# Feed-forward columns regrouped by batch in a fused attention and feed-forward kernel: the first group's opening chunks move into the cross attention, its norm onto the gate products

## The reference, cut to what matters

```python
cctx = sdpa(cq, ck, cv, causal=False)                       # 16 heads of 16
cctx = cctx.transpose(0, 2, 1, 3).reshape(b, l, CC)          # CC = 256
hidden_states = hidden_states + cctx @ cdense_w              # "dense" below
mi = rms_norm(hidden_states, ln_post_attn_w)                 # mean square over the 512 channels
v_out = jax.nn.silu(mi @ v_gate) * (mi @ v_up) @ v_down      # hidden width I = 1376
l_out = jax.nn.silu(mi @ l_gate) * (mi @ l_up) @ l_down
hidden_states = hidden_states + jnp.where(vm, v_out, l_out)
```

## Time and profile before

| what | us |
|---|---|
| three runs | 2171.53, 2175.74, 2179.38 (median 2175.74) |
| the profiled execution, and its span from first to last instruction | 2180.68, 2178.7 |
| PE busy over the span | 1996.9 (92%) |
| DVE, ACT, POOL busy | 1523.9, 1007.2, 509.4 |
| feed-forward, from its first instruction to the end of the span | 1682.3 to 2178.7 |

### The profile page before, as it was taken

One profiled execution on the slowest core, in us unless ns is written; L12 is line 12 of the kernel. 1 busy time (PEld: TensorE's weight loads), 2 busy tenths in 40 slices (PEclk: granted clock), 3 DMA queues, 4 the chain that ended last, 5 costly groups with the idle time before them and its releaser, 6 DMA issues. The chain is left out here.

```text
span 2178.7 us, 32799 instructions
## 1 busy us (share of the span) xinstructions
PE 1996.9 (92%) x12654; PEld 1340.6 (62%) x12654; DVE 1523.9 (70%) x2111; ACT 1007.2 (46%) x1748; POOL 509.4 (23%) x496
## 2 busy tenths in 40 slices
PE   6999997799979997788879999999998799999997
PEld 5788875677845554676634444444434677878885
DVE  5676776588847775656579999999952565766563
ACT  1232314455425554444348888888884222221111
POOL 0321231133401222332201312223222212221211
PEclk9999998799969999999979999999999899999998
DMA  3222112333377663685545344354401333334332
GB/s 139 71 99 80 35 57 78 121 122 122 101 189 175 169 151 103 205 254 201 154 114 96 68 89 87 73 98 78 91 14 40 112 92 99 102 109 114 94 97 56
DMA packets 174793, 236.92 MB, mean 109 GB/s; under 512 B 26218, under 2 KB 103022, under 8 KB 172426
## 3 DMA queue, kind: packets, MB, share of 16 engines
q1 hardware_dynamic: 166480, 223.65, 38.3%
q0 software_dynamic: 7856, 10.90, 1.8%
q10 hardware_dynamic: 288, 0.08, 0.0%
HBM read 169.54 MB, written 62.91 MB: 107 GB/s over the span
## 5 line engine op out<-in xcount | busy, mean ns | idle before, releaser
L2120 ACT ACTIVATE pT_x<-ps 128x512 f32<-128x512 f32 (+1 forms) x832 | 451.3, 595 | 84.6 <-PE ps L2218 57.0
L2159 DVE TENSOR_REDUCE quarters<-ps 128x2 f32<-128x804 f32 x480 | 454.1, 992 | 45.5 <-PE ps L2190 44.7
L2233 PE MATMUL ps<-pT_x,vx_ring 128*17 128x256 f32 (+1 forms) x3328 | 261.5, 387 | 0.2 <-ACT osb_x L2102 0.2
L105 PE MATMUL ps<-mi_h,w_hi 128*128 128x512 f32 (+1 forms) x440 | 174.0, 395 | 12.8 <-DVE mi_l L2414 12.8
L2379 POOL TENSOR_TENSOR sg<-sg,keep_all 128x512 f32<-128x512 f32 (+1 forms) x55 | 88.1, 1602 | 386.0 <-ACT sg L2358 386.0
L106 PE MATMUL ps<-mi_h,w_lo 128*128 128x512 f32 (+1 forms) x440 | 173.2, 394 | 0.0
L107 PE MATMUL ps<-mi_l,w_hi 128*128 128x512 f32 (+1 forms) x440 | 173.1, 393 | 0.0
L1307 DVE TENSOR_REDUCE row_max_s<-ps 128x1 f32<-128x384 f32 (+3 forms) x176 | 109.4, 633 | 68.6 <-PE ps L1339 67.8
L1279 ACT ACTIVATE pT_s<-ps 128x512 f32<-128x512 f32 (+1 forms) x176 | 96.0, 558 | 117.6 <-PE ps L1364 115.6
L99 DVE CAST w_hi<-w_raw 128x512 fp32r<-128x512 f32 (+1 forms) x165 | 84.3, 511 | 72.4 <-PE ps L107 65.4
L2233 PEld LDWEIGHTS ps<-pT_x,vx_ring 128*17 128x17 f32 (+1 forms) x3328 | 55.6, 95 | 110.7 <-issue 68.8
(11 more groups left out here) (350 smaller groups left out, 4821.0 us busy)
## 6 DMA issues: line engine op xcount, KB each, us to landing
qkv_l<-self_q_by_part SPq DMA_DIRECT2D x48, 256.0 KB, 4.4
qkv_h<-self_k_by_part SPq DMA_DIRECT2D x48, 256.0 KB, 6.7
w_raw<-L_xattn_l_gate SPq DMA_DIRECT2D x40, 256.0 KB, 2.9
w_raw<-L_xattn_l_up SPq DMA_DIRECT2D x40, 256.0 KB, 2.9
w_raw<-L_xattn_l_down SPq DMA_DIRECT2D x40, 256.0 KB, 2.7
kx_first<-cross_k_by_part SPq DMA_DIRECT2D x36, 200.2 KB, 7.2
cross_v_by_group<-v_aug SPq DMA_DIRECT2D x16, 442.0 KB, 3.9
vx_ring<-cross_v_by_group SPq DMA_DIRECT2D x16, 442.0 KB, 10.1
```

Of the source, the lines that this page charges most:

```text
L105: nc.tensor.matmul(dst, ah, bh, start=start, stop=False, **how)
L2120: nc.scalar.activation(pT[0:kn, u % 3, j, :], ps[0:kn, 5 + v % 3, :], ACT.Exp, scale=SCALE)\
L2159: nc.vector.tensor_reduce(out=quarters[:, g % 2, pair, :, q, quarter], in_=ps[:, at:at + 2, 0:MAXW], axis=AX.X, op=ALU.max)\
L2233: last = nc.tensor.matmul(ps[j * HD:j * HD + CHD + 1, 4, queries], v_r[0:kn, g % RING, kt, j, :], pT[0:kn, u % 3, j, queries], start=kt == ...
```

## The change

The stream `h_all` is laid out [P, DT, B*512] with the first 384 tokens (EARLY) of the four batches first and the four times 128 late ones last. Group 0 is now columns 0 to 511: all early tokens of batch 0 and 128 of batch 1. Group 3 stays the late tokens.

- Eight dense units (batches 0 and 1) go into steps 0 to 7 of the last group, half a unit after each half step. Those of batch 2 follow the last step. Those of batch 3 open the feed-forward stage.
- For group 0 the channel weight is put on by DVE (`first_rows`) without the token factor, the first four weight tiles are loaded early and split by DVE (`first_weights`), and PE runs the sum of squares and g0 u0 g1 u1 at the end of the cross attention (`first_chunks`). ACT makes the factor `rs_first` there.
- In group 0 the token factor goes onto the gate product on DVE (`scale_gate`) ahead of silu, and onto the mask row for the up product (`keep_first`).
- `root` and what follows it move one chunk later (AHEAD + 1). The last down product signals each of its four tiles, and SP stores each tile after its own addition.

```diff
-            early = [("dense", b, j) for b in range(groups // 4 - 1) for j in range(4)]
-            by_step.append([("flip", groups - 1)] + early + [("dense", groups // 4 - 1, j) for j in range(4)])
+            for n in range(8):
+                by_step[(groups - 1) * steps + n].append(("dense", n // 4, n % 4))
+            late = [("dense", groups // 4 - 2, j) for j in range(4)]
+            by_step.append(late[:2] + [("flip", groups - 1)] + late[2:])
...
+                        for n in range(2, RAW):
+                            load_first_tile(n)
                         sp.wait_ge(s["s_zero"], 1)
...
                         keep_sums(NG - 1)
+                        for k in range(DT):
+                            nc.scalar.activation(squares[:, k, :], h_all[:, k, 0:S], ACT.Square).then_inc(s["s_sq"], 1)
+                        act.wait_ge(s["s_tot"], 1)
+                        nc.scalar.activation(rs_first, ps[:, 1, :], ACT.Ln, bias=eps_col[:, 0:1], scale=1.0 / D).then_inc(s["s_root"], 1)
+                        act.wait_ge(s["s_root"], 1)
+                        nc.scalar.activation(rs_first, rs_first, ACT.Exp, scale=-0.5).then_inc(s["s_root"], 1)
                         high(NG // 2 - 1)
...
+                                    if o == ("dense", 1, DT - 1):
+                                        dve.wait_ge(s["s_used"], n + 1)
+                                        first_rows()
+                                        first_weights()
...
+                        def first_chunks():
+                            for k in range(DT):
+                                pe.wait_ge(s["s_sq"], k + 1)
+                                last = nc.tensor.matmul(ps[:, 1, :], ones[:, :], squares[:, k, :], start=k == 0, stop=k == DT - 1)
+                            last.then_inc(s["s_tot"], 1)
...
+                            for n in range(RAW):
+                                pe.wait_ge(s["s_fws"], n + 1)
+                                for k in range(DT):
+                                    cut = slice(k * P, (k + 1) * P)
+                                    three(ps[:, 4 + 2 * (n % 2) + n // 2, :], w_hi[:, n, cut], w_lo[:, n, cut], x_first[0][k],
+                                          x_first[1][k], k == 0, k == DT - 1)
...
+                        def scale_gate(c):
...
+                            nc.vector.tensor_tensor(out=sg[0:cn, c % 2, :], in0=ps[0:cn, 4 + c % 2, :], in1=rs_first[0:cn, :], op=ALU.mult)\
+                                .then_inc(s["s_sc"], 1)
...
-                                if c % NC == AHEAD:
+                                if c % NC == AHEAD + 1:
                                     root(i + 1)
...
+                            if scaled(c):
+                                scale_gate(c)
+                            if c == 0 and normed:
+                                add_last_batch(0)
+                                add_last_batch(1)
...
                                 for j in range(DT):
-                                    nc.vector.tensor_tensor(out=h_all[:, :, j, rows(last)], in0=h_all[:, :, j, rows(last)],
-                                                            in1=by_batch(ps[:, j, :]), op=ALU.add).then_inc(s["s_res"], 1)
+                                    if c == ALL - 1:
+                                        dve.wait_ge(s["s_end"], j + 1)
+                                    nc.vector.tensor_tensor(out=h_all[:, j, rows(last)], in0=h_all[:, j, rows(last)],
+                                                            in1=ps[:, j, :], op=ALU.add).then_inc(s["s_res"], 1)
```

More of the change, by code:

```diff
@@ L2254, in _ @@
                                 values(u - 1, 1)
-                            while todo:
-                                fill(todo.pop(0))
+                            for o in todo:
+                                if o[0] == "dense":
+                                    dense_part(o, 1)
+                                elif o != todo[0]:
+                                    fill(o)
                         for part in range(2):
@@ L2306, in store @@
                                 return
-                            sp.wait_ge(s["s_res"], DT * (i + 1))
                             for k in range(DT):
-                                sp.dma_start(out[k * P:(k + 1) * P, :, rows(i)], h_all[:, :, k, rows(i)]).then_inc(s["s_out"], 16)
+                                sp.wait_ge(s["s_res"], DT * i + k + 1)
+                                for at, batches, tokens in pieces(groups[i]):
+                                    n = tokens.stop - tokens.start
+                                    sp.dma_start(out[k * P:(k + 1) * P, batches, tokens],
+                                                 h_all[:, k, at].rearrange("p (b n) -> p b n", n=n)).then_inc(s["s_out"], 16)
                         for n, (w, c) in enumerate(tiles):
@@ L2325, in _ @@
                         store(NG - 1)
-                        sp.wait_ge(s["s_out"], 16 * DT * len(set(groups)))
+                        sp.wait_ge(s["s_out"], 16 * DT * sum(len(pieces(g)) for g in set(groups)))
                     @block.scalar
@@ L2345, in round_x @@
-                            nc.scalar.activation(x_hi[:, groups[i], k, :], full[:, k % 2, :], ACT.Copy).then_inc(s["s_nhi"], 1)
-                        if normed:
-                            for k in range(DT):
-                                square(0, k)
-                            root(0)
-                            for k in range(DT):
-                                round_x(0, k)
+                            act.wait_ge(s["s_nx"], DT * (i - 1) + k + 1)
+                            nc.scalar.activation(xs_h[groups[i]][k], full[:, k % 2, :], ACT.Copy).then_inc(s["s_nhi"], 1)
@@ L2464, in _ @@
                         if normed:
-                            for k in range(DT):
-                                pe.wait_ge(s["s_sq"], k + 1)
-                                last = nc.tensor.matmul(ps[:, 0, :], ones[:, :], sq[:, k, :], start=k == 0, stop=k == DT - 1)
-                            last.then_inc(s["s_bank"], 1)
+                            for j in range(DT):
+                                cut = slice(j * P, (j + 1) * P)
+                                for k in range(ET):
+                                    last = three(ps[:, j, :], cdh[:, k, cut], cdl[:, k, cut], last_pairs[0][:, k, :], last_pairs[1][:, k, :],
+                                                 k == 0, k == ET - 1)
+                                last.then_inc(s["s_cd"], 1)
                         for n, (w, c) in enumerate(tiles):
```

285 lines of the change are left out of this document (189 added, 96 removed).

## The result

The changed kernel takes 2164.24 us (median of 10 runs, 2160.89 to 2168.87) against 2177.38 before (10 runs): a ratio of 0.9938, 95% interval 0.9923 to 0.9952. It is faster by 13.1 us, where 30.1 were forecast. Within them the gain from the cross attention's first matmul to the end of the span is 16.8 us (1077.5 against 1060.7); the other 3.1 lie in earlier stages, which the diff does not touch.

What follows compares the result with a forecast made beforehand. PE, busy 92%, was taken as the bound, so gains come only where it stands still, mainly the seam between cross attention and feed-forward. 24.9 - 1.5 + 3.0 + 3.7 = 30.1 us off 2175.74 gives 2145.6, range 2139 to 2157.

Steps and rivals of the forecast that it cites:

- the rivals: Other outcomes: dense work not absorbed 0.10, DVE bound or late weights 0.10, no change 0.03, slower 0.02.
- dense among the steps: Last cross-attention group: three matmuls per half step make it 1.58 us instead of 1.18; last step ends 6.4 us later.
- tail on PE: After the last step: 24 dense matmuls, sums of squares and 48 matmuls take PE 19.9 us, without waiting.
- barrier: Between cross attention and feed-forward: 1.74 us, with PE ending the stage and POOL's chain 1.9 us ahead.
- feed-forward's opening to d0: Feed-forward start: batch 3's dense units and low clock take 7.2 us; first down product d0 can start at 7.7.
- low clock at 1611: After a 1.44 us PE wait the clock averaged 0.57, losing 1.7 us; the feed-forward's opening was charged likewise.
- first-group waits behind d0: Feed-forward's first group: DVE's extra work makes PE wait 1.5 us in all, ends 0.5 to 5.0.
- later `root`: Three feed-forward groups: moving it one chunk later on ACT removes a 1.0 us PE wait each, 3.0 us back.
- the end: After the last matmul: only the last addition and one store issue remain behind PE, 3.7 us back, at least 2.0.
- dense not absorbed: Rival: inserted matmuls delay ACT, each half step pays 0.69 us; 4.6 us more, 2150.2; chance 0.10.
- the transfers costed at nothing: Extra loads at cross attention's and feed-forward's starts and in the stream: no cost; 1.5 and 3 us worst at the starts.
- The first group's rounds: Feed-forward's first group: DVE round 7.1 us against PE's 8.24 per chunk, so PE stays the bound with 1.1 spare.

Runs made afterwards that it cites:

- pad_480: Changed kernel with 480 unused bytes ahead of mi_h, placing the rows within 512 bytes as in the kernel before: 2158.28 us, ratio 0.9918.
- mid_drain: Changed kernel with one more POOL drain in the middle of the last group, where POOL waits for the inverse: 2157.80 us, ratio 0.9910.
- last_sp: Changed kernel with the last group's eleven DMAs issued by SP instead of POOL: 2161.96 us, ratio 0.9935.
- after_pad: Changed kernel with 32 unused bytes ahead of mi_h: 2160.97 us, ratio 0.9930.
- dense_back: Changed kernel with the eight dense units put behind the last step again, the first weights' split ahead of them on DVE: 2163.98 us, ratio 0.9947.
- after_64: Changed kernel with nearly all high and low parts of rows and weights at a difference of 0 modulo 256 bytes: 2153.03 us, ratio 0.9888.
- both_64: Changed kernel with nearly all rows and weights at a difference of 0 modulo 256 bytes, plus POOL's added drain: 2145.53 us, ratio 0.9848.
- before_pad: Kernel before the change with 32 unused bytes ahead of mi_h: 2184.69 us, ratio 1.0038.
- pe_map: Only a product's three matmuls, without the kernels' other computation, at 16 x 16 places of weights and rows: 705 ns for three at a difference of 96.

## Why the prediction was wrong

The direction was right, the size not: 2145.6 (2139 to 2157) was forecast, 2164.24 came. None of the rivals happened. By the prediction's own terms, from the cross attention's first matmul in the two profiled executions:

| term | forecast | measured |
|---|---|---|
| dense among the steps | 6.4 later | 10.25 later (1618.27 to 1659.07 is 40.80, was 30.55) |
| tail on PE | 19.9 | 20.4 |
| barrier | 1.74 | 7.3 |
| feed-forward's opening to d0 | 7.7 | 7.9 |
| low clock at 1611 | stays | absent, 2.4 earlier |
| **d0 earlier, sum** | **24.9** | **17.1** |
| first-group waits behind d0 | 1.5 | 0.4 |
| later `root` | 3.0 back | 3.0 back |
| slower matmuls | not seen | 7.6 lost |
| the end | 3.7 back | 4.6 back |
| **sum** | **30.1** | **16.7 (16.8 measured)** |

The 7.6 us are what the feed-forward takes beyond 449.1 - 3.0 + 0.4. Pad_480 gives 6.8 of them back; the rest fits the first group's gate and up rows, which lie mostly in `kx_last`, 32 past the weights, where no pad moved them.

The 2.4 us of the low clock are luck, not the change. Behind the same wait of 1.4 us the clock fell for 3.4 us in eight of the study's twelve profiles of whole kernels, with pad_480, mid_drain and last_sp among them, and stayed up in four (after, after_pad, dense_back, after_64). Without it the profiled gain is 14.4 us, nearer to the 13.1 of the medians.

**The barrier** is the step that failed in kind: "The barrier took 1682.28 - (1679.85 + 0.69) = 1.74 us". That was what was left of it behind the last addition; under it lay 8.9 us of POOL's drain, and the sentence "If the chain were 1.9 us longer, the excess would be paid" took the chain's end for POOL's end. mid_drain shows it, where 7.3 becomes 1.9, and both_64 against after_64, where the time falls by 7.5.

**Durations taken as fixed** is the second, and with 7.6 us the largest: "One matmul of 512 columns takes (1714.88 - 1712.82) / 9 = 0.229 us at full clock" holds only for the old addresses. pad_480 shows it from one side and before_pad from the other. No row of the kernel before could show this within the feed-forward, but its earlier stages held the hint, with matmuls of 227 and 233 ns beside each other.

**Dense among the steps** had the right mechanism (PE becomes the bound) and the wrong size: 3.9 too small. The 0.33 for two score matmuls came from the earlier trace rows, where a like matmul on part of the array stands ahead of them; between other kinds they take 0.42. And a block of whole-array matmuls costs 0.2 more than 3 x 0.229. By the rows after, a half step is 1.86 instead of 1.58, which over sixteen gives 4.5; 3.9 came. The rival "dense not absorbed" had 11.0 for this term, nearer in number, but its cause, a delayed ACT, is not what happened: PE has no gap. The Trainium skill (TensorEngine Tiling (Array Packing), "Key Properties") says that changing the tiling mode drains the TensorE; 0.33 instead of 0.23 for the first dense matmul behind the values and 0.31 for the last, in the half step shown above, agree with it, and the prediction had left it out.

**What held:** no gap between last step and the end of PE's tail, the low clock after the barrier, the later `root`, the stores apart, the transfers costed at nothing. The first group's rounds stayed ahead of PE, but for one wait of 0.4 us, with less to spare than the 1.1 us forecast: 7.6 us from product to product, where 7.1 were forecast, against some 8.4 of PE for a chunk (36 matmuls of 0.233).

```profile
1700.65 0.69 DVE L2570 TENSOR_TENSOR prod<-ps,sg 128x512 f32<-128x512 f32 x1 [2.06 <-POOL sg L2497]
1708.28 0.69 DVE L2570 TENSOR_TENSOR prod<-ps,sg 128x512 f32<-128x512 f32 x1 [2.07 <-POOL sg L2497]
```

DVE met POOL as feared, but hidden behind PE: a cast in chunks 1 to 3 took 0.90 us instead of 0.42 beside POOL's sums of squares, and one split in the cross attention 2.41 instead of 0.69 while POOL issued a DMA and ran a product.

```profile
1655.18 2.41 DVE L2193 TENSOR_TENSOR w_lo<-w_raw,w_hi 128x512 fp32r<-128x512 f32 x1
```

## What to carry to other kernels

A barrier between stages waits for what each engine has left to finish, also where the page shows the engine idle; look for the drains under the line of the stage's end before you let another engine's work end first, and drain POOL where it idles. When a change adds or removes tiles, look at where the others land: compare the start-to-start time of unchanged matmuls in a stretch without waits before you look for a cause in the change's logic. Durations of matmuls are taken from a stretch with the same neighbours.

## What the runs showed of the hardware

- A 128 x 128 by 512-column matmul in fp32r takes 227 to 235 ns at full clock, set by the distance of rows and weights in SBUF modulo 256 bytes: best at 0, worst at 96 (pe_map). 32 unused bytes cost 0.38% of the kernel before (before_pad).
- POOL's drain took 7.65 us beyond its last product after 208 DMAs issued by it, all of which had landed; with a drain added 52 us ahead of it, the last one took 1.8 (mid_drain).
- A PE wait of 1.9 us at the same place left the clock at 1.00 in one run (mid_drain, 1689 to 1693) and at 0.61 for 4.4 us in another (both_64), and the wait of 1.4 us near 1610 did the same in four profiles and eight; what decides between the two was not tried.
